# Attention with four key tiles between PE's mode changes, and the division by the sums at the output projection's input

## The reference, cut to what matters

```python
def attn(x, w_q, w_k, w_v, w_o):              # b = 2, s = 2048, d = 512, 16 heads
    q, k, v = (proj(w) for w in (w_q, w_k, w_v))
    scores = jnp.einsum('bhqd,bhkd->bhqk', q, k) * SCALE
    probs = jax.nn.softmax(scores, axis=-1)
    attn = jnp.einsum('bhqk,bhkd->bhqd', probs, v)
    attn = attn.transpose(0, 2, 1, 3).reshape(b, s, d)
    return jnp.einsum('bsd,ed->bse', attn, w_o)
def ffn(x):                                   # weights are signs, HID = 2048
    hidden = relu(einsum('bsd,hd->bsh', x, sign(up)) * up_scale)
    return einsum('bsh,dh->bsd', hidden, sign(down)) * down_scale * output_scale
x = x + 0.5 * ffn(layernorm(x))
x = x + attn(layernorm(x))
x = x + 0.5 * ffn(layernorm(x))
```

## Time and profile before

| What | Value |
|---|---|
| Median of 3 runs | 3409.39 us (3407.52 to 3411.09) |
| Profiled execution, span from first to last instruction | 3407.8 us |
| PE busy | 3197.4 us (94%) |
| PE weight loads busy | 1993.8 us (59%) |
| DVE busy | 2247.1 us (66%) |
| ACT busy | 1631.6 us (48%) |
| POOL busy | 1484.4 us (44%) |
| Mean granted TensorE clock | 0.952 |

### The profile page before, as it was taken

One profiled execution on the slowest core, in us unless ns is written; L12 is line 12 of the kernel. 1 busy time (PEld: TensorE's weight loads), 2 busy tenths in 40 slices (PEclk: granted clock), 3 DMA queues, 4 the chain that ended last, 5 costly groups with the idle time before them and its releaser, 6 DMA issues. The chain is left out here.

```text
span 3407.8 us, 48947 instructions
## 1 busy us (share of the span) xinstructions
PE 3197.4 (94%) x15488; PEld 1993.8 (59%) x15488; DVE 2247.1 (66%) x3135; ACT 1631.6 (48%) x2819; POOL 1484.4 (44%) x333
## 2 busy tenths in 40 slices
PE   6999999998999999999999999999999976999999
PEld 4888887884444444444444444444444435888887
DVE  4555557776777777777777777777777704554553
ACT  4444443220555655555555555555556554343333
POOL 0000000001687877777777787776877760000000
PEclk9999999996899999999999998998999988999999
DMA  4101105545112112121121211211211012111110
GB/s 161 50 25 29 45 25 190 186 168 140 30 35 45 39 33 52 36 51 33 33 51 36 49 35 33 51 36 41 44 33 29 14 60 102 38 53 58 37 37 25
DMA packets 150999, 193.02 MB, mean 57 GB/s; under 512 B 87665, under 2 KB 88689, under 8 KB 142065
## 3 DMA queue, kind: packets, MB, share of 16 engines
q1 hardware_dynamic: 150768, 190.12, 20.3%
HBM read 121.91 MB, written 67.63 MB: 56 GB/s over the span
## 5 line engine op out<-in xcount | busy, mean ns | idle before, releaser
L809 DVE TENSOR_REDUCE att_row_max<-att_m 128x1 f32<-128x512 f32 x2048 | 1278.6, 681 | 455.7 <-PE att_m L917 454.9
L903 ACT ACTIVATE att_p<-att_s 128x512 f32<-128x512 f32 x2048 | 1080.3, 602 | 823.6 <-PE att_s L973 823.1
L798 POOL TENSOR_TENSOR att_acc<-att_acc,att_p 128x2048 f32<-128x2048 f32 x288 | 1325.5, 4602 | 283.2 <-ACT att_p L903 267.7
L917 PE MATMUL att_m<-att_k,att_q 96*128 96x512 f32 x2048 | 861.9, 428 | 96.8 <-DVE att_row_max L809 82.6
L973 PE MATMUL att_s<-att_q,att_k 98*128 98x512 f32 x2048 | 891.9, 439 | 16.8 <-issue 13.1
L973 PEld LDWEIGHTS att_s<-att_q,att_k 98*128 98x128 f32 x2048 | 402.6, 197 | 555.4 <-ACT att_p L903 254.5
L932 PE MATMUL att_o<-att_p,att_v 128*32 128x512 f32 x4096 | 579.9, 640 | 2.0 <-ACT head_raw L879 0.6
L917 PEld LDWEIGHTS att_m<-att_k,att_q 96*128 96x128 f32 x2048 | 414.4, 203 | 209.4 <-DVE att_row_max L809 125.3
L398 DVE TENSOR_TENSOR ffn_hid_lo<-ffn_hid,ffn_hid_hi 128x512 fp32r<-128x512 f32 x256 | 175.9, 687 | 433.0 <-ACT ffn_hid_hi L444 415.2
L472 PE MATMUL ffn_up<-s_hi,ffn_up_w 128*128 128x512 f32 x1024 | 402.8, 393 | 32.1 <-DVE s_lo L108 24.8
L441 ACT ACTIVATE ffn_hid<-ffn_up,up_s 128x512 f32<-128x512 f32 x256 | 175.9, 687 | 490.1 <-PE ffn_up L472 489.4
(11 more groups left out here) (93 smaller groups left out, 2310.6 us busy)
## 6 DMA issues: line engine op xcount, KB each, us to landing
s_x<-x_after_ffn SPq DMA_DIRECT2D x16, 1024.0 KB, 7.4
att_q<-q_hi SPq DMA_DIRECT2D x64, 256.0 KB, 3.9
att_k<-k_hi SPq DMA_DIRECT2D x64, 256.0 KB, 6.5
s_x<-xT SPq DMA_DIRECT2D x8, 1024.0 KB, 6.8
x_after_ffn<-s_out SPq DMA_DIRECT2D x8, 1024.0 KB, 8.9
q_hi<-qkv_o_hi SPq DMA_DIRECT2D x32, 256.0 KB, 2.1
q_lo<-qkv_o_lo SPq DMA_DIRECT2D x32, 256.0 KB, 2.3
k_hi<-qkv_o_hi SPq DMA_DIRECT2D x32, 256.0 KB, 2.3
```

The costliest lines, as they stand in the source:

```text
L798: nc.gpsimd.tensor_tensor(acc[j % 2][:], a[:], prob[kt % PR][:], ALU.add).then_inc(summed, 1)
L809: nc.vector.tensor_reduce(row_max[odd][:, qt, c:c + 1], m_ps[M_BANK[qt * QC + c]][:], axis=AX.X, op=ALU.max).then_inc(m_read, 1)
L903: nc.scalar.activation(prob[kt % PR][:, c * CH:(c + 1) * CH], s_ps[S_BANK[kt * QC + c]][:], ACT.Exp, scale=SCALE).then_inc(exp_done, 1)
L917: nc.tensor.matmul(m_ps[M_BANK[i]][:], q_st[b][0:KQ, qt * P:(qt + 1) * P], k_st[b][0:KQ, c * CH:(c + 1) * CH], start=True, stop=True).then ...
```

## The change

Three things, all in attention and what follows it.

1. PE's order. The key tiles run in groups of `G` = 4: 16 scores and 16 maxima with no narrow matmul between them, then the four `out_tile`s of the group before, back to back. `pooled_sums` and `transpose_max` stand at the end of such a narrow stretch. The reader of `m_ps` and `s_ps` and the three banks of each stay as they are. The tiles summed by PE are now 5, 8, 11, 14 and 15.
2. The maxima. `neg_max` is transposed unsplit; DVE takes the high part from PSUM by a cast (`neg_hi`) and the low part by a subtraction that reads PSUM (`neg_lo`). Both stand behind the reduce of unit c = 1 of tile 12, and PE's maximum c = 2 of that tile waits for them.
3. The division. `raw` is stored undivided (`store_out`); the inverses go to a table `inv_all` of 16 x 4096 in memory. `scale` leaves the heads. `OProj.load` also loads the inverses, each row spread over the 32 partitions of its head by four DMAs, and `OProj.scale` on DVE multiplies the 128 x 2048 chunk before it is split. ACT's `copy_out` stands behind the exponential of unit c = 1 of tile 4, `copy_sums` behind that of unit c = 1 of tile 8, and DVE's `invert` behind tile 8's four reduces. The last head's sums and stores end within the attention phase.

```diff
-    LEAD, LAG = 4, 2
+    LEAD, G = 4, 4
+    NG = KT // G
-    POOLED = (0, 1, 2, 4, 5, 7, 8, 10, 11, 13, 14)
-    UNPOOLED = 3
+    POOLED = (0, 1, 2, 3, 4, 6, 7, 9, 10, 12, 13)
+    DIRECT = tuple(kt for kt in range(KT) if kt not in POOLED)
...
+    def store_out(self, eng, H, row, col):
+        eng.wait_ge(self.out_copied, H + 1)
         for c in range(QC):
+            eng.dma_start(self.att[bass.ds(row, HD), bass.ds(col + c * CH, CH)], self.raw[c * HD:(c + 1) * HD, :]).then_inc(self.out_stored, 16)
+
+    def move_sums(self, eng, H, head, col):
+        eng.wait_ge(self.sums_copied, H + 1)
+        eng.dma_start(self.sums_scr[:, :], self.total[0:P:HD, :]).then_inc(self.sums_moved, 16)
+        eng.wait_ge(self.sums_moved, 32 * H + 16)
+        if not isinstance(H, int) or H > 0:
+            eng.wait_ge(self.divided, H)
+        eng.dma_start(self.tot_t[:], self.sums_scr.rearrange("a (b c) -> (a b) c", c=KT)).then_inc(self.sums_moved, 16)
+        eng.wait_ge(self.divided, H + 1)
+        eng.dma_start(self.inv_all[bass.ds(head, 1), bass.ds(col, SEQ)].rearrange("a (b c) -> (a b) c", c=KT),
+                      self.inv_t[:]).then_inc(self.inv_stored, 16)
 
     def invert(self, dve, H):
-        dve.wait_ge(self.moved, PER_HEAD * H + 32)
+        dve.wait_ge(self.sums_moved, 32 * H + 32)
+        if not isinstance(H, int) or H > 0:
+            dve.wait_ge(self.inv_stored, 16 * H)
         self.nc.vector.reciprocal(self.inv_t[:], self.tot_t[:]).then_inc(self.divided, 1)
 
-    def scale(self, dve, H):
-        dve.wait_ge(self.moved, PER_HEAD * H + 48 + 16 * QC)
-        self.nc.vector.tensor_tensor(self.fin[:], self.raw[:], self.inv_b[:], ALU.mult).then_inc(self.divided, 1)
...
     def load(self, sp, m):
         sp.dma_start(self.st.norm.cent[:], chunk(self.att, m)).then_inc(self.loaded, 16)
+        if not isinstance(m, int) or m > 0:
+            sp.wait_ge(self.scaled, m)
+        per = P // HD
+        for i in range(per):
+            src = self.inv_all[i::per, bass.ds(m * CH, CH)]
+            sp.dma_start(self.inv_b[i * HD:(i + 1) * HD, :, :],
+                         src.unsqueeze(0).to_broadcast([HD, DT, CH])).then_inc(self.loaded, 16)
+
+    def scale(self, dve, m):
+        dve.wait_ge(self.loaded, OP_LOADS * (m + 1))
+        self.nc.vector.tensor_tensor(self.st.norm.cent[:], self.st.norm.cent[:], self.inv_b[:], ALU.mult).then_inc(self.scaled, 1)
...
+                def rows_out(h, again):
                     dve.wait_ge(neg_pe, h + 1)
-                    if wait:
+                    if again:
                         dve.wait_ge(neg_loaded, 32 * h)
-                    nc.vector.tensor_copy(neg_rows[:], t_bank[0:2 * KT, 0:P]).then_inc(neg_dve, 1)
+                    nc.vector.tensor_copy(neg_hi[:], t_bank[0:KT, 0:P]).then_inc(neg_dve, 1)
+                    dve.wait_ge(neg_dve, NEG * h + 2)
+                    nc.vector.tensor_tensor(neg_lo[:], t_bank[0:KT, 0:P], f32(neg_hi[:]), ALU.subtract).then_inc(neg_dve, 1)
...
+                            if not (first and j == 0) and kt == 8:
+                                head_out.invert(dve, H - 1)
...
+                                if c == 1 and not (first and j == 0):
+                                    if kt == G:
+                                        act.wait_ge(p_used, PR + KT * H)
+                                        head_out.copy_out(act, H - 1, o_ps)
+                                    if kt == 2 * G:
+                                        act.wait_ge(t_ready, H)
+                                        head_out.copy_sums(act, H - 1, t_ps)
...
+                        for u in range(NG):
+                            for kt in range(G * u, G * u + G):
+                                step_max = not (last and (j == NB - 1 or (j == NB - 2 and kt + LEAD >= KT)))
+                                b, qt = ((j + 1) % NB, kt + LEAD) if kt + LEAD < KT else ((j + 2) % NB, kt + LEAD - KT)
+                                T = KT * (H + 1) + kt + LEAD
+                                if step_max and kt == KT - LEAD:
+                                    pe.wait_ge(loaded[b], PER * (g + 1 + (j + 2) // NB))
+                                for c in range(QC):
+                                    scores(H, j, kt, c)
+                                    if step_max:
+                                        if kt == TURN and c == 2:
+                                            pe.wait_ge(neg_dve, NEG * (H + 2))
+                                        maxima(b, T, qt, c)
+                            for kt in range(G * u - G, G * u):
+                                if kt >= 0:
+                                    out_tile(H, j, kt)
+                                elif not (first and j == 0):
+                                    out_tile(H - 1, (j - 1) % NB, KT + kt)
+                            if u == 1 and not (first and j == 0):
+                                pooled_sums(H - 1, (j - 1) % 2)
+                            if G * u + G == TURN and not (last and j == NB - 1):
+                                pe.wait_ge(m_read, MR + UNITS * (H + 2))
                                 transpose_max(H + 1)
```

## The result

The change makes the kernel slower: 3500.71 us in the median (3481.83 to 3508.17) against 3410.24 us for the kernel before on the same chip, a ratio of 1.0251, with a 95% interval of 1.022 to 1.0282. The forecast was 3475 us within 3427 to 3528. So 66 us more were forecast and 90 came.

A forecast was written before the change was run, and what follows sets the result against it. PE was taken to bound a head most of the time. Heads going from 59.7 to 61.1 us gave +43, attention's end +6, feed-forward +11 and +6: from 3407.8 to a forecast of 3475 us, range 3427 to 3528.

The forecast's parts named there:

- (f): Behind PE's idle in each head: low clock for 3 to 7 us, costing 0.65 to 1.65 us, taken as 1.15.
- (h): Start of second feed-forward: inverses' load taken as 3.3 us, then a 2.29 us multiply; +11 us in all.
- (i): Six further feed-forward chunks: split 5.6 us later, ACT's idle covering 4.21, PE losing about 1.0 each; +6 us.
- (a): PE in each head: 4 mode changes instead of 16, 12 x 0.32 = -3.8 us.
- (c): Bunched pairs in each head: DVE's 0.60 us reduces hold up PE's 0.47 us pairs, +1.34 four times, +5.4 us.
- (b): Each head: scale and the cast of the negated maxima leave DVE, -5.4 us.
- (d): After tile 8 of each head: DVE's reciprocal waits for the sums' two transfers, +2.75 us; PE idle some 2.8.
- (e): Tile 12 of each head: maximum c = 2 waits for rows_out's cast and subtraction, +1.1 us; transpose +0.2.
- (g): End of attention: the last head's sums, reciprocal and store must end before the next phase begins, +6 us.
- The clock falls often: Rival: low clock again and again in the heads' thinned stretches, +4.7 us x 31, 3621 us; chance 0.07.
- Faster, without the wait: Rival: no wait of the reciprocal in the heads and no low clock behind it, 3355 us; chance 0.09.
- The subtraction waits for POOL: Rival: rows_out's subtraction waits for POOL as scale did, up to 4.6 us x 31, 3618 us; chance 0.04.

The follow-up runs named there:

- the last pair: Changed kernel with early rows_out and inverses ahead, reduces reading 256 of 512 columns: four tiles (reciprocal behind tile 10) 3170.02 us, one tile between mode changes 3257.59 us.
- one tile, mends in: Changed kernel with G = 1, rows_out ahead of tile 12's first reduce and inverses loaded a chunk ahead: 3292.86 us, ratio 0.9656 to the kernel before.
- the later inversion: Changed kernel with only DVE's reciprocal moved from behind tile 8 to behind tile 10: 3377.18 us, ratio 0.9898 to the kernel before.
- the mended kernel with two tiles: Changed kernel with G = 2, rows_out ahead of tile 12's first reduce and inverses loaded a chunk ahead: 3297.09 us, ratio 0.9662 to the kernel before.

## Why the prediction was right, and where its sizes were off

Direction, range and the mechanism were right. The terms that were mis-sized are the low clock in (f), the last head, and the inverses' load in (h) and (i); two smaller errors of the count come first.

**The count of heads.** The 60.3 us of the prediction spread the time over all 32 heads, but the last, without maxima, is shorter (47.4 us to its last score); heads 0 to 30 take 60.6 before. And the sum takes 1.4 us x 31, where head 0 has no head before it whose sums it could wait for. Before, its cast cost it as much as the division the others; after the change it has neither, and it goes from 61.3 to 54.6 us. So the 31 heads lost 34.8 us and not 43, although the other 30 lost 1.4 each as forecast.

The terms in the prediction's own order:

**(a) and (c), the mode changes and DVE's pace.** They were forecast to nearly cancel, the first quarters of a head at 14.37 and 13.50 us (the stretch of 9.02, four or more bursts behind it). After the change these two quarters take 14.51 and 13.55 in the mean of heads 1 to 30, and with the reduces halved the stretch falls to PE's own 7.70 where ACT has no copy. Shown, as is the reason. The twelve mode changes are worth 3.2 us a head by the last pair, not quite the 3.8 of (a), and what is missing is in the two stretches that ACT then bounds. The Trainium skill, "TensorEngine Tiling (Array Packing)", Performance Considerations, says that tiling does not speed up the emptying of PSUM, which may become the bottleneck. It speaks of tiled matmuls, and the pairs here are untiled; but the trace agrees in this, that the emptying binds the bunched stretches, one reduce in 0.60 us against a pair in 0.47, for 101 us in all.

**(b) the division off DVE.** The 4.90 us instructions are gone. The sum put the whole loss down to `scale` and what follows it and named the cast of the maxima only in passing; head 0 before, with the cast and no division, shows that both had to go. That their 5.4 us a head would come back whole was too much to say: with the grouping undone the clean 54.3 is not reached (one tile, mends in: 56.4 in the mean). Of the 2.1 us between, 0.75 are DVE's pace (23 us over 31 heads) and some 0.4 the loop (the mean lies that much above the median); with the reduces halved, tiles 1, 5 and 11 are still 0.2 to 0.3 us longer than clean ones, tile 11 with the transpose.

**(d) the reciprocal's wait.** Forecast: sums issued at 2.2 us after tile 8's first score, landed at 5.7, PE idle some 2.8. The rows above: issued at 1619.30 - 1617.16 = 2.14, the second transfer 1.78 behind, the reciprocal at 1622.81, so 5.65; PE idle 2.25. It occurs in each of the heads 1 to 30, always in tile 9. Its price is 2.3 us a head, not 2.75: the two heads after the change without a low stretch behind the pause (18 and 26) take 59.7 and 59.8 us, and a head with the later inversion 57.5 in the median. Shown by the trace, and by the 123.5 us of the run without it.

**(e) `rows_out`.** The subtraction for which the trace of before had no row takes 278 ns. The idle time in tile 12 is 1.25 us, forecast 1.3:

```profile
1574.08 0.27 DVE L831 CAST att_neg_hi<-att_m 16x128 fp32r<-16x128 f32 x1
1574.38 0.28 DVE L833 TENSOR_TENSOR att_neg_lo<-att_m,att_neg_hi 16x128 fp32r<-16x128 f32 x1
```
```profile
1574.80 0.50 PE L910 MATMUL att_m<-att_k,att_q 96*128 96x512 f32 x1 [1.25 <-DVE att_neg_lo L833]
```

Its rival, that it waits for POOL as the division did, cannot be told in this kernel, where an add of POOL runs beside it in one head of 32; it is refuted below.

**(f) the clock.** The fall came, in 28 of the heads 1 to 30, but its price was taken too low. Third and fourth quarter were 17.4 (13.50 + 2.75 + 1.15) and 15.5 (14.37 + 1.1), a little more with the transpose, and take 18.13 and 15.81. Wait and clock together cost 62.0 - 57.7 = 4.3 us a head (means of heads 1 to 30, after the change and with the later inversion); less the wait's 2.3, the clock costs 2.0 instead of 1.15. Low stretches of up to 10.2 us occur, where 3 to 7 was taken. Heads 1 to 30 come to 62.0 in the mean against 60.6 before: +1.4, the forecast to the tenth. That is in part luck: (d) was 0.45 too high and (f) 0.85 too low, and both sides of the difference lie 0.9 above their figures.

**The last head** was put at "no change", since ACT paces it before and after. It took 8.2 us more (14.4 less the 6.2 of (g)). This step failed: that one engine paces both says nothing of where the bursts fall. 3.8 us come up to the last score (51.1 instead of 47.4): a stretch of sixteen scores takes 7.85 to 8.9 us at ACT's pace, and the bursts, which could fill PE's gaps, stand behind all sixteen. The other 4.4 come behind the last score, where the bursts of the last four tiles still stand. The clock falls in this head too (0.80).

**(g) the end of attention** was +6 and is +6.2: from the end of the copy of the last sums (2833.83), over their two transfers, to the next phase's first load it is 6.5 us, where before the load came 0.4 behind that copy.

```profile
2833.23 0.60 ACT L209 ACTIVATE head_total<-att_t 128x512 f32<-128x512 f32 x1 [0.26 <-PE att_t L938]
```
```profile
2834.78 0.54 SPq L218 DMA_DIRECT2D prob_sums<-head_total  x1
...
2840.36 0.39 SPq L256 DMA_DIRECT2D s_cent<-attention_out  x1
```

**(h) and (i), the inverses' load.** This is the term that was most off in all. Its size was taken as 3.3 us, "nearer to the pair issued together", and it is 5.7. The multiply starts 11.0 us after the attention load's issue (2976.86 to 2987.89), where the split started 5.3 after it before. In order, SP, DVE and PE of the second chunk after the start:

```profile
2976.86 0.41 SPq L256 DMA_DIRECT2D s_cent<-attention_out  x1
2977.37 2.40 SPq L262 DMA_DIRECT2D op_inv_b<-prob_inverse  x4
```
```profile
2987.89 2.29 DVE L267 TENSOR_TENSOR s_cent<-s_cent,op_inv_b 128x2048 f32<-128x2048 f32 x1 [4.43 <-DMA op_inv_b<-prob_inverse]
```
```profile
2993.33 0.50 PE L490 MATMUL ffn_up<-s_hi,ffn_up_w 128*128 128x512 f32 x1 [3.30 <-ACT ffn_hid_hi L462]
2996.60 0.63 PE L286 MATMUL s_mean<-s_hi,wo_hi 128*128 128x512 f32 x1
```

The split is 5.7 + 2.3 = 8.0 us later; ACT's 4.21 us of idle cover only so much of it, and 3.8 are left, of which PE stands idle 3.30, after which its matmuls come at the lower clock. That is 4.8 us a chunk instead of 1.0, 29.1 instead of 6 for six, and 16.4 instead of 11 at the start. The prediction had the upper end of this (some 28) among its bounds and took a value near the lower. A cover of 4.21 us against a cost of 5.6 is a cliff: each further microsecond of the load counts in full (2.4 more load, 3.8 more a chunk), and that should have drawn the estimate upwards.

**The signs.** Idle in tile 9, the reciprocal's wait, maxima 0.60 apart and stretches of 9 us all came; of attention's end and the start of the feed-forward phase 17 us were forecast and 22.6 came.

**The rivals.** The clock stays up (3439): refuted in the heads by the row at 0.51. The clock falls often (3621): refuted in heads with maxima, true in the last head. Faster, without the wait (3355): the wait is there, but the mechanism was right: taking it away gives 3377. Mode change not the cost (3593): refuted by the last pair. The subtraction waits for POOL (3618): refuted.

## What to carry to other kernels

Before work is grouped to save an engine's switching, divide the group's length by the pace of the engine that empties its results: here sixteen pairs at 0.60 us behind three banks cost as much as the twelve mode changes saved (101 us against 99), and the order of time before already had both numbers. Look at the last round by itself: it has another bound, and the grouping lost 10 us there. When an instruction is regrouped, list what is queued behind every instruction that now stands nearer to its input; one reciprocal two tiles too early was 123 us of 3500, as much as the best of these kernels gains on the kernel before (118). When an instruction that stalls is taken off an engine, look at the next one on that engine that could stall in the same way. And where a cost is just above its cover, measure or bound the cost from its upper end.

## What was not expected of the hardware

**The clock can fall without a long pause.** In the last head, which has scores and no maxima, four tiles at a time go at ACT's pace, and PE's pauses are of half a microsecond or less. In the kernel with the later inversion the order of time on PE has there:

```profile
2641.01 6.67 PE L904 MATMUL att_s<-att_q,att_k 98*128 98x512 f32 x13 [0.28 <-ACT att_p L881]
...
2656.88 0.98 PE L904 MATMUL att_s<-att_q,att_k 98*128 98x512 f32 x2 [0.48 <-ACT att_p L881]
```

and the stretches of the last head are, for this kernel and then for the mended one with one tile:

```profile
2647.00:2690.00 43.00, 40.15 (x174) 14.20 (x174) 0.25 (x1) 23.98 (x48) 37.09 (x9) 0.78 0.03 7
```
```profile
2610.00:2650.00 40.00, 35.49 (x195) 12.10 (x187) 0.25 (x1) 27.73 (x54) 38.81 (x9) 1.00 0.03 7
```

The mended kernel with two tiles lies between:

```profile
2602.00:2657.00 55.00, 50.70 (x227) 16.41 (x223) 0.25 (x1) 31.88 (x64) 43.14 (x11) 0.88 0.02 6
```

The same matmuls keep 1.00 when a burst stands between every four scores, give 0.88 when it stands between every eight and 0.78 between every sixteen. Longer pauses are not what does it: up to its last score the kernel at 1.00 has the longer ones (up to 0.79 us, 6.0 in all) and the one with four tiles the shorter (up to 0.49, 3.1 in all). The Trainium skill, "TensorE: Matmul & The Clock Gate", A second HAM failure mode, says that a PE which idles briefly and often as it cycles through PSUM banks can swing between both levels. The last head with four tiles agrees with it, and the heads with maxima, 1.00 at a pair every 0.60 us, do not. What separates the two was not tried.

**A subtraction with one input in PSUM does not wait for POOL.** The division, with both inputs in SBUF, took 4.90 us beside POOL's adds and 0.68 alone. The subtraction reads one input from PSUM and one from SBUF, and in the mended kernel with one tile it takes the same 278 ns in all 32 heads, 31 times while an add of POOL was running (its line: number, ns min/median/max, first and last start; then DVE and POOL in order of time, POOL's seven adds merged):

```profile
L839 DVE TENSOR_TENSOR att_neg_lo<-att_m,att_neg_hi x32: 278/278/280, 845.1 to 2591.4; 16x128 fp32r<-16x128 f32 x32
```
```profile
1575.91 0.28 DVE L839 TENSOR_TENSOR att_neg_lo<-att_m,att_neg_hi 16x128 fp32r<-16x128 f32 x1
```
```profile
1545.23 32.54 POOL L818 TENSOR_TENSOR att_acc<-att_acc,att_p 128x2048 f32<-128x2048 f32 x7
```

The size of the instruction is not what decides: the cast of 128 x 16 in the kernel before, with its input in SBUF, took 4.21 us beside POOL's add in head 0, and 174 ns with no add running. That it is the place of the operands was not tried by itself.
